# The common order of two instruction streams, read from a table of run lengths in place of a greedy list scheduler

## The reference

```python
x = layernorm(x + two_attentions(x))     # 16 heads of 8, 4 kv heads: causal over 1024 with a latent kv, then a window of 32
x = layernorm(x + experts(x))            # softmax gate over 8 experts, the top 2; gelu(x W1[e] + b1[e]) W2[e] + b2[e], 128 -> 512 -> 128
x = layernorm(x + linear_attention(x))   # elu + 1 features, 64 wide, running sums over the sequence
x = layernorm(x + two_layers(x))         # each: token shift, 8 heads of 64 in blocks of 64 that look one block back, then a gated gelu layer
```

## Time and profile before

| what | us |
|---|---|
| median of three runs (lowest, highest) | 2703.6 (2696.78, 2711.81) |
| the profiled execution's own time | 2702.28 |
| its span, first to last instruction | 2700.2 |
| PE busy, share of the span | 1829.8, 68% |
| DVE, ACT, POOL busy | 1295.1, 1155.6, 724.7 |
| mean granted TensorE clock | 0.799 of full |

### The profile page before, as it was taken

How to read it: one execution, slowest core, us unless ns; L and a number is a source line. 1 busy time by engine, 2 the same in 40 slices (tenths; PEclk the granted TensorE clock), 3 DMA queues, 4 the chain that set the end, 5 groups by cost and what they waited for, 6 DMA issues and landing times.

```text
span 2700.2 us, 37744 instructions
## 1 busy us (share of the span) xinstructions
PE 1829.8 (68%) x13975; PEld 1182.0 (44%) x13975; DVE 1295.1 (48%) x2580; ACT 1155.6 (43%) x2706; POOL 724.7 (27%) x634
## 2 busy tenths in 40 slices
PE   1864455389866785559867665738986667668776
PEld 1123354234344573334434564524434556445454
DVE  3124114754276325566366513575436632557574
ACT  1642131267643352157844333137764334225553
POOL 0420210164222411145231312027331142023241
PEclk8676586689878697779987687769996778768998
DMA  3000250000000250000000241000000034000000
GB/s 116 1 1 1 86 168 3 8 13 13 5 9 21 90 166 9 12 13 13 5 12 15 66 152 55 4 12 17 9 8 5 13 113 150 6 14 18 13 21 13
DMA packets 52935, 99.06 MB, mean 37 GB/s; under 512 B 11423, under 2 KB 26003, under 8 KB 52627
## 3 DMA queue, kind: packets, MB, share of 16 engines
q1 hardware_dynamic: 48659, 88.26, 11.1%
q0 software_dynamic: 4096, 8.40, 1.1%
HBM read 66.02 MB, written 13.83 MB: 30 GB/s over the span
## 4 chain that ended last, share of the span: by engine, by line
PE 39%; DVE 27%; ACT 10%; issue 9%; POOL 7%; DMA 4%; SPq 2%; another core or an unknown queue 1%; DVEq 0%; POOLq 0%; ACTq 0%
PE PH L765 4%; PE PB L1166 3%; PE PB L1146 3%; PE PB L1082 2%; DMA front_arena<-in_W 2%; POOL front_arena L2043 2%; ACT back_arena L1418 2%; PE PH L996 2%; PE PD L809 2%; PE PB L1202 2%; ACT front_arena L1277 2%; DVE back_arena L1924 2%; PE PD L985 2%; POOL fy L2101 2%; POOL x_rows L2061 1%
## 5 line engine op out<-in xcount | busy, mean ns | idle before, releaser
L1277 ACT ACTIVATE front_arena<-PD 128x1024 f32<-128x1024 f32 (+3 forms) x384 | 304.7, 821 | 140.8 <-PE PD L809 139.2
L2096 POOL TENSOR_TENSOR back_arena<-back_arena 128x512 f32<-128x512 f32 x128 | 165.0, 1291 | 556.9 <-DVE back_arena L1924 556.8
L2043 POOL TENSOR_TENSOR front_arena<-front_arena,tri 128x256 f32<-128x256 f32 x256 | 202.1, 802 | 373.6 <-ACT front_arena L1277 372.7
L1146 PE MATMUL PB<-wqkv,hT 128*128 128x512 f32 x384 | 236.3, 705 | 36.1 <-DVE back_arena L1924 18.6
L1418 ACT ACTIVATE back_arena<-PB,fnm 128x128 f32<-128x128 f32 x512 | 180.9, 371 | 122.3 <-DVE fnm L1931 122.2
L765 PE MATMUL PH<-front_arena 128*32 128x512 f32 (+3 forms) x1536 | 182.7, 551 | 62.1 <-POOL front_arena L2043 39.8
L1931 DVE TENSOR_REDUCE fnm<-PB 128x4 f32<-128x512 f32 x128 | 88.4, 691 | 280.3 <-PE PB L1166 279.5
L2101 POOL TENSOR_TENSOR fy<-fm,minus_half 128x16 f32<-128x16 f32 x64 | 190.3, 2974 | 106.8 <-DVE fm L1947 105.5
L1953 DVE TENSOR_TENSOR back_arena<-back_arena,frd 128x512 f32<-128x512 f32 x128 | 162.6, 1271 | 4.4
L1166 PE MATMUL PB<-back_arena 64*64 64x128 f32 x2048 | 156.3, 297 | 0.0
L1767 DVE COPY front_arena<-PH 128x256 f32<-128x256 f32 (+1 forms) x48 | 19.8, 414 | 276.6 <-PE PH L996 276.6
(11 more groups left out here) (273 smaller groups left out, 3799.8 us busy)
## 6 DMA issues: line engine op xcount, KB each, us to landing
front_arena<-in_W SPq DMA_DIRECT2D x60, 514.0 KB
W<-in_W SPq DMA_DIRECT2D x32, 514.0 KB
back_arena<-back_arena SPq DMA_DIRECT2D x128, 128.0 KB
y_rows<-front_arena SPq DMA_DIRECT2D x20, 256.0 KB, 5.5
front_arena<-x_rows SPq DMA_DIRECT2D x8, 512.0 KB, 4.3
X<-in_L_attn_hidden SPq DMA_DIRECT2D x64, 32.0 KB, 1.9
out_y<-Nb SPq DMA_DIRECT2D x64, 32.0 KB, 1.6
front_arena<-x_rows SPq DMA_DIRECT2D x4, 448.0 KB, 5.3
```

The costliest lines, as they stand in the source:

```text
L1146: pe.matmul(p, hT[:, 128 * i:128 * i + 128], wqkv[:, l, c:c + 512], start=True, stop=True).then_inc(filled(b, "f" + n, l, i), 1)
L1277: act.activation(pb[:, :, 0:n], p[:, :, 0:n], ACT.Exp, scale=INV_SQRT_HD).then_inc(freed(b, "S", half, g, kc, jp), 1)
L2043: pool.tensor_tensor(pb, pb, tri[:, :].unsqueeze(1).to_broadcast([128, 2, 128]), ALU.mult).then_inc(sg("masked"), 1)
L2096: pool.tensor_tensor(T1[k % 2][:, hs, :], T1[k % 2][:, hs, :], T2[:, hs, :], ALU.add).then_inc(sg("rot"), 1)
```

## The change

Two edits. The body of `order()` no longer computes: it expands a string of 618 numbers, which are the lengths of alternating runs of front and back steps, beginning with the front. The greedy list has 1048 runs. The hand-written costs are no longer read. And on DVE one `link(ins)` (an increment on the last rotary product and a wait of DVE for it) moves from behind the step `qn` 0 to ahead of it, still in the step `rope` 7.

```diff
+RUNS = """
+234 1 4 1 2 1 9 1 1 2 3 1 3 2 1 3 2 1 1 3 8 1 2 3 1 1 1 1 2 1 7 1 2 4 1 5 1 3 3 1 1 9 1 1 1 1 2 2 1 3 2 2 2 2 1 1 2 1 1 1 1 4 1 5 2 2 1 2 2 1 1 2 2 1
...
+"""
 def order():
 
-    streams = {"F": FRONT, "B": BACK}
...
-        soonest = min(o[0] for o in options)
-        start, _, who = min((o for o in options if o[0] <= soonest + 0.05), key=lambda o: o[1])
...
+    at, out = {"F": 0, "B": 0}, []
+    for n, run in enumerate(RUNS.split()):
+        who = "FB"[n % 2]
+        for _ in range(int(run)):
+            out.append((who, at[who]))
+            at[who] += 1
+    assert at == {"F": B * len(FRONT), "B": B * len(BACK)}, at
     return out
@@
                             ins = dve.tensor_tensor(tmp[:, t, :, :, s], sw[:, t, :, :, 1 - s],
...
+                    link(ins)
                     yield front_at(b, "qn", a, 0)
-                    link(ins)
                     link(dve.tensor_tensor(QR, QR, arena_rope, ALU.add))
```

More of the change, by code:

```diff
@@ L266 @@
 assert len(F_AT) == len(FRONT) and len(B_AT) == len(BACK)
-def order():
-    streams = {"F": FRONT, "B": BACK}
[L272 to L294, removed]
-        soonest = min(o[0] for o in options)
-        start, _, who = min((o for o in options if o[0] <= soonest + 0.05), key=lambda o: o[1])
[L297 to L309, removed]
+RUNS = """
[9 rows of a table added]
+"""
+def order():
+    at, out = {"F": 0, "B": 0}, []
[5 more added lines that the diff above has]
+    assert at == {"F": B * len(FRONT), "B": B * len(BACK)}, at
     return out
```

## The result

The kernel after takes 2594.18 us, the median of four runs (2576.22 to 2601.41); the kernel before took 2700.86 beside it (2696.78 to 2711.81). The ratio is 0.9589, 95% interval [0.9529, 0.9649]: 107 us, where 37 were forecast. The direction was right.

The account below looks back on a forecast made before the run. No engine alone was taken as the bound, but two chains of short dependent steps sharing in-order engines. Section terms -20 + 13 - 29 + 3 + 50 - 10 - 18 - 26 gave -37 us, forecast 2666 us, range 2612 to 2728.

Parts of the forecast that it names:

- the hold: ACT's idle wait in section I, 12.2 us a round, 36.6 in three; forecast midway between staying and going.
- B: Section nearly bound by PE: three more back steps, +3 us; 17 fewer table loads, -10 us.
- D: Section where DVE is busy 33.5 of 47.7 us: gains ten back steps at 1.29, +13 us.
- J: Section of each round whose back-step count is even over the three rounds: no change forecast.
- E: Section where back steps fill PE's holes: loses 48 steps at 0.61, -29 us.
- A: Section set by DVE's chain: loses 17 back steps at 1.20, -20 us.
- H: The experts' section: gains 24, 21 and 21 back steps, PE should end it, +50 us.
- I: Section with the gather: loses 21 back steps; -8 us if the hold stays, -45 if it goes, -26 taken.
- G: Section of the sixteen scatters: fewer POOL back operations between them, spans of 26.0, 20.5 and 23.5 us, -18 us.
- second rival: Steps taken from E and A were filling holes and give back nothing: +12 us, 2714 us, chance 0.15.
- third rival: Experts' product, gelu, product in H becomes serial, H above about 91 us a round: +37 us, 2739 us, chance 0.15.
- first rival: The hold goes each round, H packs densely, B's loads come off, D's steps are covered: -84 us, 2618, chance 0.25.

Follow-up runs that it names:

- the even order: The kernel after with the same number of back steps per section, spread evenly in all sections but J: 2683.25 us against 2663.52 before, ratio 1.0073.
- the later pair: The kernels before and after, both unchanged, repeated and profiled later: after 2569.71 us against 2660.37 before, ratio 0.9658.
- the run with A even: The kernel after with the back steps of section A alone spread evenly: 2583.2 us, ratio to before 0.9722.
- the exchange: The kernel after with 20, 10 and 18 back steps of section H put back into E at even distances: 2598.79 us, ratio to before 0.9776.
- the runs without loads: Both gelus replaced by an exponential, all table loads but one gone: searched order 2560.9 us, ratio 0.9644; evenly spread order 2659.43 us, ratio 0.9997 to before.
- the one with G even: The kernel after with the back steps of section G alone spread evenly: 2592.3 us, ratio to before 0.9743.

## Why the prediction was wrong in its size

**The step that failed** is the pricing itself, "I count how many back steps enter or leave each section over three rounds and price them by the row of that section". Its own counts, at even places, gave 1.0073. Without the hold's share the forecast was about -19 us, the even order measured +20 and the searched one -91. The text named the place of single steps as what would prove it wrong, but expected to see it in B, D and J, "over 15 us a round"; B of round one did change by 17, and by 13.5 in the later pair. 113 us lie between two placings of the same counts, more than the whole result. What the counts are worth isn't a number of its own: at even places they lost, and within the searched list 48 steps moved back to E cost 29 us.

Of the 70 us that the sum lacks without the hold, A makes 23, E 21, H and D 18 together, I 7 and B 4, while G takes 2 back.

Term by term, the sum had:

- **A, -20; measured -43** in both pairs. A mean price over 12 steps (1.20) stood for what 4 to 7 steps gave back at 2.5 each; by the run with A even, steps among the rope and the norm make PE's long wait longer (13.9 to 19.9 us). And a section's length is no price where both streams go on into the next one: in the greedy order A's gain came back in B.
- **E, -29; measured -46**, all in rounds one and three, and -50 in the later pair. 0.61 was a mean; the exchange shows 1.27 for the last 20 and 18, and 0 for round two's 10. The second rival, "the cheap slots are lost", is refuted by it for rounds one and three. Its sign, 95 us in round two, did come in the first profile, but there the clock was low (last section); repeated it is 89.4, the "near 89" of the forecast.
- **H, +50; measured +29, and +41 in the later pair.** The mechanism was right: H filled up, 68.53 of 73.70 us. But the 24 steps added 17.7 us of PE (68.53 less the 50.81 of the earlier trace rows), 0.74 each, not 1.09 or 0.93. Among the 28 in H are four of the `q`, `k`, `v` projections and none of the gated layer, which may be why; no run shows it. PE's idle time in H came down from 10.3 to 5.2 us, where the working left 2.5 (84.5 less 82.0). Repeated, with the clock at 0.96 in place of 1.00, a step is 0.86 (70.98 less 50.45 over 24). The third rival, the serial chain, needed over 91 us; H was never above 77 in the kernel after.
- **G, -18; measured -14**, with the scatters' spans within 2 us of the forecast; round two fell short most, 31.8 us where 28.7 were forecast.
- **Table loads in B, -10.** B as a whole changed by -10 against -7 forecast, but not by this term: the runs without loads show no gain in B. They price the 57 loads at 9 us, 8 of them in H, which the sum had as covered. The Trainium skill ("ScalarE: Activation LUTs", section "What ACT_TABLE_LOAD costs") adds a drain of about 1380 ns to each switch; none shows in the rows above (0.3 us idle before 18 loads), and H with its 25 loads did not become the dearer rival.
- **Section I, -26; measured -38.** Without holds on either side it went from 125.6 to 110.9, so the 21 steps were worth 15, not 8, and the hold in it 24 by the profile, where I took 18. The half was near by luck: both ends, "stays" and "goes", supposed that the order decides, and it is there or not with the same order.
- **D, +13; measured +4.** J, the head and the tail: 0, and -2, -4 and -2 measured. The link: 0, and open (above).

The first rival, "the holds go and the fill is dense", was nearest in its sum, 2618 against 2594, and had a chance of 0.25. Much of that is luck: 37 of its 84 us were the holds, and without them it says -47, where 91 were measured. Its reasons were half right: the fill in H is dense and D's ten steps were mostly covered, while no relief of B by its table loads shows.

## What to carry to other kernels

Where two streams share in-order engines, a table of "steps in a section times the section's mean price" doesn't give the time: with the same table the kernel was 0.7% slower or 3.4% faster. Look instead at the longest wait of each section, ask which step of the other stream stands ahead of it on that engine (a POOL sum between two indirect DMAs, a DVE product in the rope), and whether it can stand elsewhere. Where rounds repeat the same work, run the best round's list in all of them before searching further, and look at each round: here one gained 23 us and another lost 7.

## What the runs showed of the hardware that was not expected

**One program, two clocks in the same section.** Section E of rounds one and two holds the same instructions in the same order in the kernel after and in the one with G even (G comes behind). Here are the two sections in the first, then in the second, then the first 5 us of E in each.

```profile
781.20:852.40 71.20, 52.78 (x502) 39.20 (x501) 35.78 (x90) 22.25 (x49) 5.45 (x3) 0.73 0.02 5
1371.90:1461.30 89.40, 71.59 (x591) 53.09 (x590) 46.11 (x104) 28.17 (x66) 10.93 (x7) 0.66 0.03 7
...
781.20:786.20 5.00, 4.05 (x71) 2.23 (x70) 0.00 (x0) 3.96 (x4) 0.00 (x0) 0.98 0.01 3
```

```profile
776.10:853.40 77.30, 59.36 (x503) 43.91 (x503) 35.85 (x90) 22.36 (x49) 5.52 (x4) 0.65 0.02 5
1375.00:1470.20 95.20, 77.76 (x588) 55.60 (x584) 46.34 (x106) 28.17 (x66) 11.22 (x7) 0.59 0.03 6
...
776.10:781.10 5.00, 5.00 (x63) 2.47 (x64) 0.00 (x0) 3.07 (x3) 0.00 (x0) 0.64 0.02 3
```

In both PE had stood idle in D for some 10 us, the clock had come down to 0.50 (1.2 GHz), and PE had begun again within the 10 us ahead of E. In the one the granted clock was 0.98, nearly all at 2.4 GHz, in the first 5 us of E; in the other it was 0.64 and then 0.50 for five more us. The section is 6 us longer with it, in round one and in round two. What decides between the two isn't shown. So single profiles differ by more than their order: in E of round two of the kernel after, 95.3 us in its first profile, the clock was 0.59 in the mean, and 0.66 when it was 89.4.

**A hold that comes and goes with one kernel.** In the execution at 2702 us PE, DVE and ACT all stood still for 9 to 11 us in section I of every round, while POOL issued the gather's indirect DMAs; in the profile at 2660 us, with the same kernel, never. I is 40 us shorter there over the three rounds, as much as the whole forecast. The cause is open, the chip included.
